# A graph network kernel on one core: register loads of window bases without their run-time bound check

## The chip, the cores and the metric

The kernel runs on one core of one Trainium2 chip. The metric is the time of one execution on the device in microseconds (us). Three runs of the kernel before took 7002.58, 7008.87 and 7010.35 us; their median is 7008.87 us.

## The reference

The input is a node matrix x (6250 nodes, 128 features, float32) and 206250 edges (src, dst), sorted by dst. Cut to what matters:

```python
def _L0_gnn_ref(x, edge_index, ...):
    row, col = (edge_index[0], edge_index[1])
    e_in = concatenate([x[row], x[col]], axis=-1)
    ef = relu(e_in @ ei_w1 + ei_b1) @ ei_w2 + ei_b2
    ew = sigmoid(ef @ ew_w + ew_b)[:, 0]
    out1 = _layernorm(gelu(_gcn(x, W1, b1, row, col, ew)), ln1_g, ln1_b)
    cat = concatenate([out1[row], out1[col], ef], axis=-1)
    ef = _layernorm(ef + (relu(cat @ eu_w1 + eu_b1) @ eu_w2 + eu_b2), lne_g, lne_b)
    ew = sigmoid(ef @ ew_w + ew_b)[:, 0]
    return _layernorm(gelu(_gcn(out1, W2, b2, row, col, ew)), ln2_g, ln2_b)
h = maximum(_layernorm(x), 0.0)
x = x + _L0_gnn_ref(h, ...)          # edge weights, two weighted sums over edges
h = maximum(_layernorm(x), 0.0)
x = x + _L1_gnn_ref(h, ...)          # an unweighted mean over edges, then a linear layer
```

`_gcn` takes for every destination node the sum over its edges of norm times the source node's row, where norm is the edge's weight times the inverse square roots of the weighted degrees of both ends.

## The kernel before, in words

The edges are cut into 404 groups of 512, and four groups make a step, so a pass over all edges has 101 steps. As the edges are sorted by destination, a group touches a short run of neighbouring destination nodes: a window of 32 nodes that begins at the group's base. The 404 bases lie as integers in one row, `base_sb`. Whoever reads a window from a table in HBM, or adds to a window of the accumulator `acc`, needs the base in a register of its own engine. `bases_of(eng, it)` (L830) loads the four bases of step `it` into registers of the engine `eng`; the library call behind it takes `min_val` and `max_val`.

The stages, in the order of the program, each ended by a barrier over all engines (`end_stage`, L326):

- setup: tables of node rows and the relative indices;
- **first edge round** (`edge_round(False)`, L835): for each group POOL issues four indirect DMAs (`gather_rows`, L791, L812) that gather the source rows of 128 edges each; ACT loads the group's destination window by DMA (`windows_of`, L1107), makes a one-hot matrix and TensorE (PE) multiplies it with the window (`q_of`, L1069); DVE adds, weighs and reduces to edge weights; SP writes the gathered rows to `kept_d`. ACT calls `bases_of` twice in a step, DVE once (L958), and DVE adds degrees into `acc` at the bases (`add`, L946);
- **first sum round** (`sum_kept_round`, L1212): the kept rows are read back, PE sums them by window, ACT copies the sums out of PSUM (`stage_folded`, L1287, L1290) and POOL calls `bases_of` once a step (L1408) and adds four windows into `acc` (L1413);
- the node update between the rounds;
- **second edge round** (`edge_round(True)`): the same gathers with wider rows; PE does `t_of`, `z_of` and `u_of` (L1003 to L1045) in turn, ACT does two relus for a group (`relus`, L1151: L1155 releases the matmul of `u_of` at L1029, L1158 releases `z_of`) and loads windows two steps ahead; ACT calls `bases_of` once a step, at the step's start (L1167), DVE once (L958);
- **second sum round**, and a node update;
- **count round** (`count_round`, L1424): 31 batches of 26 groups of 256 edges. DVE makes one-hots, PE counts and multiplies, ACT copies the 26 groups' sums to `staged_sums` (`stage_sums`, L1502, L1505), POOL loads the bases in fours (a load of its own, L1529, seven for a batch, the last of two) and adds 26 narrow windows one after the other (L1534), each waiting for the one before;
- the last linear layer.

POOL may issue gathers for a group once the group two steps earlier is used (`used`: L1029's semaphore in the second edge round, L892's in the first) and kept. The last step of a stage has no other work beside it: ACT stages the last sums, then POOL adds them, then the barrier comes.

Of the kernel before, what the change touches and what calls it, by code (L numbers as in the profile page):

```python
# [11 lines left out]
ds = bass.ds  # L12
SP = mybir.EngineType.SP
DVE = mybir.EngineType.DVE
POOL = mybir.EngineType.Pool
ACTE = mybir.EngineType.Activation

def build(nc, x, src, dst, W1, b1, W2, b2, ln1_g, ln1_b, ln2_g, ln2_b, ei_w1, ei_b1, ei_w2, ei_b2,
# [6 lines left out]
    NPAD = NT * P  # L25
# [4 lines left out]
    U = 4  # L30
# [4 lines left out]
    WIN = 32  # L35
    MAXR = N // WIN + 1
    NALL = NPAD + WIN
# [6 lines left out]
    CG = 26  # L44
# [16 lines left out]
    def done(i):  # L61

        return i + 1 + CREDIT

    ctx = ExitStack()
    with ctx:
# [113 lines left out]
        base_sb = sb("base_sb", [1, QG], I32)  # L180
# [649 lines left out]
        def bases_of(eng, it):  # L830

            return nc.values_load_multi_w_load_instructions(
                base_sb[0:1, ds(it * U, U)], engines=(eng,), min_val=0, max_val=NALL - WIN)[1]

        def edge_round(update):  # L835
            width = PR if update else ED
# [6 lines left out]
            with nc.Block() as block:  # L843
# [23 lines left out]
                def _(dve):  # L867
# [86 lines left out]
                    def step(it, par, k, behind, last):  # L954

                        if behind > 1:
                            keep_weights(it - 2)
                            firsts = bases_of(DVE, it - 2)  # L958
                        for u in range(U):
                            if update and not (last and u >= U - 2):  # L960
                                if u + 2 < U:
                                    hotT_of(it, par, k, u + 2)
                                else:
                                    hotT_of(it + 1, 1 - par, k + par, u + 2 - U)
                            if behind > 0 and u == U - 1:
                                weigh_hot(it - 1)
                            take_z(it, par, u)
                            if behind > 1 and u < 2:
                                add(it - 2, 2 * u, firsts[2 * u])
                                add(it - 2, 2 * u + 1, firsts[2 * u + 1])  # L970
                            if behind > 0 and u == 0:
                                hot_of(it - 1)
                            if behind > 0 and update and u == 1:
                                scale(it - 1)
                        if update:
                            variance(it)
# [17 lines left out]
                    for it in (STEPS - 2, STEPS - 1):  # L994
                        keep_weights(it)
                        firsts = bases_of(DVE, it)
                        for u in range(U):
                            add(it, u, firsts[u])
                            if it < STEPS - 1 and u == 0:
                                hot_of(it + 1)  # L1000
                                weigh_hot(it + 1)
# [101 lines left out]
                def _(act):  # L1103
# [13 lines left out]
                    def first_windows(it, par):  # L1117
                        firsts = bases_of(ACTE, it)
                        for u in range(U):
                            windows_of(it, par, u, firsts)  # L1120
# [303 lines left out]
        def count_round():  # L1424
# [3 lines left out]
            with nc.Block() as block:  # L1428
                @block.vector
                def _(dve):  # L1430
                    link = chain(dve, s_dve)
                    dve.sem_inc(s_hit, CREDIT)
                    link(nc.vector.tensor_scalar(rawz[:, :], rel[:, :], 0.0, None, ALU.is_ge))
                    link(nc.vector.scalar_tensor_tensor(rawz[:, :], rel[:, :], float(CW - 1), rawz[:, :],
                                                        ALU.is_le, ALU.mult))
                    link(nc.vector.tensor_tensor(code[:, :], srct[:, :], rel[:, :], ALU.add))
                    link(nc.vector.tensor_tensor(code[:, :], code[:, :], rawz[:, :], ALU.mult))
                    with dve.Fori(0, CB) as b:
                        for g in range(CG):
                            i = b * CG + g  # L1440
                            dve.wait_ge(s_built, done(i - 2))
                            for j in range(2):
                                nc.vector.tensor_scalar(hit_p[:, g % 2, j, :], part_ids[:, :],  # L1443
                                                        ew[:, ds(i * 2 + j, 1)], None, ALU.is_equal)
                                last = nc.vector.tensor_scalar(hit_c[:, g % 2, j, :], cell_ids[:, :],  # L1445
                                                               code[:, ds(i * 2 + j, 1)], None, ALU.is_equal)
                            last.then_inc(s_hit, 1)
# [73 lines left out]
                @block.gpsimd  # L1521
                def _(pool):
                    pool.sem_inc(s_acc, CREDIT + CG)

                    def batch(b, par):
                        pool.wait_ge(s_staged, done(b))
                        for g0 in range(0, CG, U):
                            n = min(U, CG - g0)
                            firsts = nc.values_load_multi_w_load_instructions(  # L1529
                                base_sb[0:1, ds(b * CG + g0, n)], engines=(POOL,), min_val=0, max_val=NPAD)[1]  # L1530
                            for g in range(g0, g0 + n):
                                a = acc[:, ds(firsts[g - g0], CW)]
                                pool.wait_ge(s_acc, done(b * CG + g - 1 + CG))
                                nc.gpsimd.tensor_tensor(a, a, staged_sums[:, par, g * CW:(g + 1) * CW],  # L1534
                                                        ALU.add).then_inc(s_acc, 1)
                    with pool.Fori(0, CB // 2) as q:
                        batch(2 * q, 0)
                        batch(2 * q + 1, 1)
                    batch(CB - 1, 0)
# [705 lines left out]
```

## Time and profile before

| | us |
|---|---|
| median of three runs | 7008.87 |
| lowest, highest | 7002.58, 7010.35 |
| span of the profiled execution | 8159.6 |
| first edge round in it (window 149 to 2665) | 2516 |
| first sum round (2714 to 3331) | 617 |
| second edge round (3437 to 6332) | 2895 |
| second sum round (6379 to 7018) | 639 |
| count round (7141 to 8114) | 973 |

The span is the only time the profiled execution gives; it is 1150.7 us above the median of the timed runs. Busy shares over the span are PE 59%, DVE 47%, POOL 45%, ACT 35%; no engine is busy throughout. Register instructions, waits and DMA issues don't count as busy; where they are shown, the engine's name has a q behind it (POOLq). The ends of matmuls are modelled.

### The profile page before, as it was taken

Reading aid. Unit: us, or ns where it says so; the run is one execution under the profiler, and the core shown is the slowest. Engines: PE = TensorE matmul, PEld = TensorE weight load, DVE = VectorE, ACT = ScalarE, POOL = GpSimd, SP = SyncE. Lnnn points to the kernel's source line nnn. Section 1 sums busy time; section 2 is a strip of 40 time slices with the busy share of each in tenths; the row PEclk is TensorE's granted clock in tenths of the full one; section 3 lists DMA queues with packets and bytes.
Section 4 is the critical chain, followed back from the end, with each engine's and each line's share of the span. In section 5 each row is a group of like instructions: output and inputs, shape, how many; then the busy total and the mean of one; then the engine's idle time right before and its main releaser. Section 6 shows DMA issues by size and latency. Waiting matters only on the chain. (4 is left out here: it accounts for less than half of the span.)

```text
span 8159.6 us, 171241 instructions
## 1 busy us (share of the span) xinstructions
PE 4819.1 (59%) x41016; PEld 3544.0 (43%) x41016; DVE 3862.8 (47%) x17284; ACT 2873.1 (35%) x5415; POOL 3652.2 (45%) x5091
## 2 busy tenths in 40 slices
PE   2111111111111588588888888888888588599997
PEld 1000000000000476455555555555555476478886
DVE  3222222222223788533333333333333688788886
ACT  2222222222222455322322222222223455566664
POOL 3566666666666011255555555555554011411222
PEclk6555555555555667777777777777778666699998
DMA  4455555555555477455555555555555577200000
GB/s 124 133 142 138 139 139 140 141 139 142 141 140 138 150 222 220 139 160 161 166 161 165 159 161 162 162 160 161 161 159 136 149 221 219 96 1 0 0 0 32
DMA packets 1010949, 1117.36 MB, mean 137 GB/s; under 512 B 216892, under 2 KB 749475, under 8 KB 1010440
## 3 DMA queue, kind: packets, MB, share of 16 engines
q1 hardware_dynamic: 652056, 516.07, 21.3%
q0 software_dynamic: 155136, 423.83, 19.7%
q10 hardware_dynamic: 203680, 176.57, 7.7%
q8 instruction: 31, 0.51, 0.0%
q14 instruction: 46, 0.38, 0.0%
HBM read 877.11 MB, written 238.87 MB: 137 GB/s over the span
## 5 line engine op out<-in xcount | busy, mean ns | idle before, releaser
L812 POOL DMA_INDIRECT counts<-tab_pr,idx x1616 | 1552.4, 961 | 1285.2 <-PE pu L1029 709.9
L812 POOL DMA_INDIRECT counts<-tab_p,idx x1616 | 1553.2, 961 | 926.5 <-issue 565.1
L1069 PE MATMUL pz<-tmpb,pieces 96*128 96x64 bf16 x1616 | 139.4, 236 | 2005.7 <-issue 1009.9
L1069 PEld LDWEIGHTS pz<-tmpb,pieces 96*128 96x128 bf16 x1616 | 94.7, 121 | 2077.9 <-issue 2077.9
L886 DVE BATCH_NORM_STATS2 st<-pz 128x6 f32<-128x64 f32 x1616 | 252.7, 219 | 1532.0 <-remote 850.2
L1029 PE MATMUL pu<-pieces,tmpb 96*128 96x512 f32 x808 | 628.9, 871 | 392.4 <-ACT pieces L1155 271.1
L892 DVE TENSOR_TENSOR pieces<-counts,pz 128x256 f32<-128x256 f32 x404 | 168.9, 418 | 1373.1 <-remote 1242.8
L1127 ACT ACTIVATE pieces<-pieces,iota_third 96x512 f32<-96x512 f32 x404 | 290.1, 718 | 1457.4 <-issue 1323.4
L1039 PE MATMUL pz<-wz,pieces 96*128 96x65 f32 x3232 | 732.9, 313 | 91.9 <-ACT pieces L1158 90.7
L1040 PE MATMUL pz<-wv,pieces 128*128 128x65 f32 x3232 | 713.8, 307 | 0.0
L1413 POOL TENSOR_TENSOR acc<-acc,pieces 128x32 f32 x808 | 199.7, 247 | 1124.9 <-issue 1018.8
L1470 PE MATMUL pz<-counts,pieces 128*128 128x286 bf16 x4557 | 682.5, 284 | 0.1
L1039 PEld LDWEIGHTS pz<-wz,pieces 96*128 96x128 f32 x3232 | 570.9, 221 | 214.3 <-ACT pieces L1158 114.4
L1158 ACT ACTIVATE pieces<-pu,eub 128x512 f32<-128x512 f32 x404 | 277.7, 687 | 1085.9 <-PE pu L1029 702.2
L1040 PEld LDWEIGHTS pz<-wv,pieces 128*128 128x128 f32 x3232 | 577.8, 223 | 0.0
L1445 DVE TENSOR_SCALAR pieces<-cell_ids,tmpb 128x540 bf16<-128x540 f16 x1612 | 572.1, 355 | 0.2 <-issue 0.2
L1534 POOL TENSOR_TENSOR acc<-acc,staged_sums 128x11 f32 x806 | 190.6, 236 | 785.6 <-issue 669.3
L1155 ACT ACTIVATE pieces<-pt 64x512 f32<-64x512 f32 x404 | 237.6, 588 | 775.4 <-remote 356.3
L1470 PEld LDWEIGHTS pz<-counts,pieces 128*128 128x128 bf16 x4557 | 442.0, 97 | 101.4 <-ACT counts L1497 0.4
L1443 DVE TENSOR_SCALAR pieces<-part_ids,ew 128x128 bf16<-128x128 bf16 x1612 | 407.4, 253 | 158.1 <-PE pt L1459 87.1
L1275 ACT ACTIVATE pieces<-counts,neg_p 128x512 f32<-128x512 bf16 x404 | 291.7, 722 | 491.0 <-DMA counts<-srcp_d 472.8
L1374 DVE SCALAR_TENSOR_TENSOR pieces<-iota_t,srct,pt 128x98 f32<-128x98 f32 x1616 | 399.6, 314 | 94.5 <-PE pt L1320 93.7
(318 smaller groups left out, 9906.9 us busy)
## 6 DMA issues: line engine op xcount, KB each, us to landing
kept_d<-counts SPq DMA_DIRECT2D x808, 256.0 KB
counts<-kept_d SPq DMA_DIRECT2D x808, 256.0 KB
pieces<-rel_d ACTq DMA_DIRECT2D x808, 192.0 KB
counts<-srcp_d SPq DMA_DIRECT2D x808, 64.0 KB
counts<-tab_p,idx POOLq DMA_INDIRECT x1616
counts<-tab_pr,idx POOLq DMA_INDIRECT x1616
tmpb<-tab_q ACTq DMA_DIRECT2D x808, 12.0 KB
tmpb<-tab_s ACTq DMA_DIRECT2D x404, 16.0 KB
```

The lines of the kernel that those rows point to most:

```text
L812: pool.indirect_dma_start(out=rows[:, par, u, j, 0:width], out_offset=None, in_=table, in_offset=bass.IndirectOffsetOnAxis(ap=idx[:, 2 * h ...
L886: nc.vector.bn_stats(st16[:, u * SUB + j, :], z[:, j, 0:ED])
L1029: nc.tensor.matmul(pu[u % 2][:, :], win[0:WE, par, u, :], tT[0:WE, u, :], start=False, stop=True, skip_group_check=True).then_inc(s_u, 1)
L1039: nc.tensor.matmul(o, tT[0:WE, u, j * P:(j + 1) * P], wz[0:WE, :], start=True, stop=False)
L1040: last = nc.tensor.matmul(o, uT[:, u % 2, j * P:(j + 1) * P], wv[:, :], start=False, stop=True)
L1127: nc.scalar.activation(apart, rel_row[:, par, u, :], ACT.Square, bias=iota_third[0:TRI, 0:1], scale=-1.0).then_inc(s_sq, 1)
L1158: nc.scalar.activation(uT[:, u % 2, :], pu[u % 2][:, :], ACT.Relu, bias=eub1[:, 0:1]).then_inc(s_urelu, 1)
L1275: nc.scalar.activation(dist, srcp_row[:, slot, :], ACT.Square, bias=neg_p[:, 0:1]).then_inc(s_sq, 1)
L1374: last = nc.vector.scalar_tensor_tensor(junk[:, u * SUB + j, :], iota_t[:, :], srct[:, ds(i * SUB + j, 1)], looked[u][:, j * HT:(j + 1) * ...
L1443: nc.vector.tensor_scalar(hit_p[:, g % 2, j, :], part_ids[:, :], ew[:, ds(i * 2 + j, 1)], None, ALU.is_equal)
L1445: last = nc.vector.tensor_scalar(hit_c[:, g % 2, j, :], cell_ids[:, :], code[:, ds(i * 2 + j, 1)], None, ALU.is_equal)
L1470: last = nc.tensor.matmul(pz[par][:, 0:CN], h3[:, k, t, :], counts[:, par, t, :], start=(t == 0 and k == 0), stop=(t == NT - 1 and k == 2))
```

## The change

Both calls that load bases into registers, `bases_of` (first and second edge round, sum rounds) and the load in `count_round`, get the argument that leaves out the check of each loaded value against `min_val` and `max_val` at run time. The loads stay, and so do all other instructions and their order.

```diff
         def bases_of(eng, it):
 
             return nc.values_load_multi_w_load_instructions(
-                base_sb[0:1, ds(it * U, U)], engines=(eng,), min_val=0, max_val=NALL - WIN)[1]
+                base_sb[0:1, ds(it * U, U)], engines=(eng,), min_val=0, max_val=NALL - WIN,
+                skip_runtime_bounds_check_because="next_windows and the end of a sum round clamp every base to NPAD")[1]
...
                             firsts = nc.values_load_multi_w_load_instructions(
-                                base_sb[0:1, ds(b * CG + g0, n)], engines=(POOL,), min_val=0, max_val=NPAD)[1]
+                                base_sb[0:1, ds(b * CG + g0, n)], engines=(POOL,), min_val=0, max_val=NPAD,
+                                skip_runtime_bounds_check_because="the end of a count round clamps every base to NPAD")[1]
```

In the program, a load of four bases is one TENSOR_LOAD, and eight sequencer instructions stand behind it (rows "ISA x8"): for each base one that compares (FUSED_REGOPS in the trace) and one that asserts (SEQ_ASSERT). The top of ACT's loop in the second edge round, before:

```order
L1190 UNCONDITIONAL_BRANCH
L1190 ISA
L832 TENSOR_LOAD base_sb
L832 ISA x8
L1153 ISA
L1154 REGISTER_ALU
L1155 ACTIVATE pieces<-pt 64x512
```

and with the change (its lines stand one or two further down):

```order
L1191 UNCONDITIONAL_BRANCH
L1191 ISA
L832 TENSOR_LOAD base_sb
L1154 ISA
L1155 REGISTER_ALU
L1156 ACTIVATE pieces<-pt 64x512
```

The eight instructions between the load and the first relu of the step are gone. POOL's loop in the count round, before:

```order
L1529 ISA
L1529 TENSOR_LOAD base_sb
L1529 ISA x8
L1533 REGISTER_ALU
L1534 ISA
L1534 TENSOR_TENSOR acc<-acc,staged_sums 128x11
```

and with the change:

```order
L1530 ISA
L1530 TENSOR_LOAD base_sb
L1535 REGISTER_ALU
L1536 ISA
L1536 TENSOR_TENSOR acc<-acc,staged_sums 128x11
```

Here the eight stood between the load and the first add of each four. On no engine does any other instruction appear, vanish or change its place.

## Rows read from the trace of the kernel before

**Rows 1.** Head of the profile page.

```profile
span 8159.6 us, 171241 instructions
```

**Rows 2.** By stretch: length, PE, PEld, DVE, ACT, POOL busy; PEclk, DMA share, GB/s.

```profile
149.00:2665.00 2516.00, 326.83 (x2828) 168.50 (x2828) 692.45 (x1919) 568.02 (x910) 1564.52 (x1667) 0.50 0.53 140
...
3437.00:6332.00 2895.00, 2388.84 (x11716) 1638.54 (x11716) 1049.74 (x4351) 830.73 (x1213) 1563.56 (x1667) 0.75 0.57 160
7141.00:8114.00 973.00, 936.24 (x7781) 752.80 (x7781) 772.18 (x3228) 586.26 (x1644) 190.61 (x806) 0.98 0.00 0
```

**Rows 3.** Instructions of L832: count, min/median/max ns, first and last start.

```profile
L832 ACTq SEQ_ASSERT  x1208: 1/18/1400, 150.5 to 6257.7; - x173
...
L832 DVEq FUSED_REGOPS  x808: 7/190/1392, 237.8 to 6329.3; - x162
```

**Rows 4.** Instructions of L1529, same columns.

```profile
L1529 POOLq FUSED_REGOPS  x1016: 51/147/162, 7205.3 to 8112.1; - x170
L1529 POOLq SEQ_ASSERT  x806: 18/18/24, 7206.0 to 8112.3; - x162
```

**Rows 5.** POOL's adds at the end of the count round, timeline (start, us).

```profile
8095.69 0.21 POOL L1534 TENSOR_TENSOR acc<-acc,staged_sums 128x11 f32 x1 [0.17 <-POOL acc L1534]
...
8110.23 0.21 POOL L1534 TENSOR_TENSOR acc<-acc,staged_sums 128x11 f32 x1 [1.19 <-issue]
...
8112.89 0.21 POOL L1534 TENSOR_TENSOR acc<-acc,staged_sums 128x11 f32 x1 [0.17 <-POOL acc L1534]
```

**Rows 6.** ACT's last staging copy of the count round, timeline.

```profile
8091.82 0.41 ACT L1505 ACTIVATE staged_sums<-pz 128x286 f32<-128x286 f32 x1 [17.79 <-PE pz L1470]
```

**Rows 7.** End of the first sum round, ACT and POOL, timeline.

```profile
3325.93 0.28 ACT L1290 ACTIVATE pieces<-pd 128x128 f32<-128x128 f32 x1 [1.17 <-PE pd L1342]
...
3327.78 0.24 POOL L1413 TENSOR_TENSOR acc<-acc,pieces 128x32 f32 x1 [0.17 <-POOL acc L1413]
3329.20 0.25 POOL L1413 TENSOR_TENSOR acc<-acc,pieces 128x32 f32 x1 [1.17 <-issue]
```

**Rows 8.** DVE at the ends of the two edge rounds, timeline.

```profile
2658.77 0.18 DVE L952 TENSOR_TENSOR acc<-acc,pd 33x32 f32 x1 [1.19 <-PE pd L1057]
...
6326.66 0.69 DVE L938 TENSOR_TENSOR pieces<-pieces,wts 128x512 f32<-128x512 bf16 x1
```

**Rows 9.** ACT's last sigmoid of the second edge round, timeline.

```profile
6325.62 0.31 ACT L1148 ACTIVATE wts<-zl,zb 128x16 f32<-128x16 f32 x1
```

**Rows 10.** Instructions of L812, count, min/median/max ns, first and last start.

```profile
L812 POOL DMA_INDIRECT counts<-tab_p,idx x1616: 943/949/1455, 150.8 to 2639.9; - x180
L812 POOL DMA_INDIRECT counts<-tab_pr,idx x1616: 943/949/1467, 3438.7 to 6285.7; - x180
```

**Rows 11.** One gather of POOL in the first edge round, timeline.

```profile
1500.81 0.95 POOL L812 DMA_INDIRECT counts<-tab_p,idx  x1 [0.30 <-issue]
```

**Rows 12.** Who waited for whom: us in total, times, longest us.

```profile
POOL counts L812 <- PE pu L1029: 709.9, 221, 6.5
...
PEld pu L1029 <- ACT pieces L1155: 285.2, 92, 6.5
```

**Rows 13.** A step's boundary in the second edge round, ACT, timeline.

```profile
5004.15 0.69 ACT L1158 ACTIVATE pieces<-pu,eub 128x512 f32<-128x512 f32 x1 [2.60 <-PE pu L1029]
5004.30 0.32 ACTq L1109 DMA_DIRECT2D pieces<-rel_d  x1
...
5007.17 0.59 ACT L1155 ACTIVATE pieces<-pt 64x512 f32<-64x512 f32 x1 [2.33 <-issue]
```

**Rows 14.** PE at the same boundary, timeline.

```profile
5001.71 1.08 PE L1029 MATMUL pu<-pieces,tmpb 96*128 96x512 f32 x2
...
5007.81 2.08 PE L1029 MATMUL pu<-pieces,tmpb 96*128 96x512 f32 x2 [0.92 <-ACT pieces L1155]
```

**Rows 15.** Two stretches of the second edge round, columns as rows 2.

```profile
5160.00:5440.00 280.00, 237.81 (x1128) 163.61 (x1128) 100.02 (x419) 79.93 (x117) 151.11 (x161) 0.73 0.57 159
5440.00:5720.00 280.00, 229.41 (x1167) 156.24 (x1166) 103.63 (x431) 82.49 (x121) 155.31 (x165) 0.79 0.58 163
```

## The prediction

> **What bounds the kernel now.** First the times: the profiled execution spans 8159.6 us [rows 1], the runs take 7008.9, so 1150.7 us of the span are not in the runs, and I must say where they lie before I price anything. The sum below is made as differences, which I subtract from the median. The views by stretch [rows 2] show two edge rounds of 2516 and 2895 us; all the rest is 8159.6 - 5411 = 2748.6 us. If the rest is as long in the runs, both edge rounds together take 7008.9 - 2748.6 = 4260 us there.
>
> Next, the floor of an edge round. POOL issues 1616 gathers in each [rows 10], each 0.95 us long with 0.30 us before the next [rows 11]: 1616 x 1.25 = 2020 us. The first starts 1.8 us into each window of rows 2, and the last starts 25 us (2665 - 2639.9) and 46 us (6332 - 6285.7) before the end, so the two rounds can't be shorter than 4040 + 4 + 71 = 4115 us. The runs have 4260: they go nearly at POOL's pace, and at most about 145 us are waits of POOL. In the profile it waits much more, in the second round 709.9 us for the matmul of L1029 alone [rows 12]. I read this as: the edge rounds are POOL's in the runs, with a remainder in the second round, where PE and ACT are coupled. The count round is PE's (936 of 973 us busy, [rows 2]), with POOL behind it; at the end of each stage the last engine works alone.
>
> **The price of a check.** Each loaded base costs one comparison and one assertion on its engine's instruction stream: 147 + 18 ns on POOL [rows 4]; on DVE the comparison is 190 ns, and ACT's assertion is 18 ns too [rows 3]. Four bases are thus at least 4 x 0.165 = 0.66 us. From above: an add of POOL behind a load waits 1.19 us against 0.17 without one [rows 5], so load and checks together add 1.02 us. I take 0.9 us for four, since the load runs largely beside the add before it, and 1.0 on DVE. The change removes 1208 checked values on ACT [rows 3], 808 on DVE, 808 on POOL in the sum rounds and 806 on POOL in the count round [rows 4]: by 0.225 us each over 800 us of instruction stream. Hardly any of it sets an end, as follows. It removes nothing else, adds nothing, and moves no DMA past a queue.
>
> These instructions don't occupy the compute part: while ACT's relu runs from 5004.15 for 0.69 us, its stream already issues a DMA at 5004.30 [rows 13]. The Trainium skill, "Perfetto Trace Analysis", section "Per-instruction lifecycle", says the same of DVE and ACT: the stream hands an instruction to a wait queue and goes on to the next one. By that rule alone, a check behind a running instruction would be free wherever the engine has a queue of work; the sum would then be the ends of the stages only, which is my second rival.
>
> **Count round.** The checks are 5.9 us for a batch (26 values). In the steady state POOL waits for the next batch, and they cost nothing: PE covers them, and would if they were twice as long. At the end they don't hide. ACT has staged the last sums at 8091.82 + 0.41 = 8092.2 [rows 6], POOL finishes the batch before at 8095.69 + 0.21 = 8095.9, then does the last one until 8113.1 [rows 5]. Without checks the earlier batch is 5.9 us shorter, so the last starts at 8092.2 (3.7 us earlier) and is itself 5.9 shorter: -9.6 us. Late next is ACT's copy.
>
> **Sum rounds.** POOL has one load in a step of 6.1 us (617 / 101) and waits in the steady state; DVE, PE and the row reads cover it, so 0. At the end the last sums are staged at 3325.93 + 0.28 = 3326.2, POOL ends the step before at 3327.78 + 0.24 = 3328.0, and its next add is held 1.17 us [rows 7]. Two earlier steps without checks remove the 1.8 us of backlog, the last saves 0.9; since the load already runs beside the add before it, I take 2.5 us. Two rounds: -5.0 us.
>
> **Ends of the edge rounds.** DVE loads bases for the last two steps, and for one more while it still has groups to do. In the first round two such loads lie in DVE's chain (1.19 us before the add at 2658.77 [rows 8] is one): -2.0 us. The third is followed by a wait for PE's last sums and gives nothing. In the second round the weighing at 6326.66 [rows 8] follows the sigmoid that ends at 6325.93 [rows 9], so only 0.7 can come off. Together -2.7 us. At the start ACT's loads have two steps of POOL's work (40 us) before anyone misses them: 0.
>
> The ends sum to 9.6 + 5.0 + 2.7 = **-17.3 us**, to 6991.6.
>
> **Edge rounds, steady.** First round: in a step ACT drops the checks of eight values (1.8 us), DVE of four (1.0 us), of the 20 us that POOL takes. PE is busy for 13% of it. Taken at 0. Second round: ACT's load stands between the window DMAs and the first relu of a step (L1155), which L1029 needs. At 5007.17 this relu starts after 2.33 us idle, and PE waits 0.92 us for it [rows 13, 14]: about what the checks take. If that held for all 101 steps it would be 91 us. PE's weight load at L1029 waits for L1155 in 92 of 404 groups [rows 12], 23%. I take 0.23 x 101 x 0.9 = -21 us; the bounds are 0 and -91. The release of POOL by L1029 then comes earlier, and late next are POOL's own gathers. DVE's checks I cost at nothing: PE doesn't wait for DVE in these rows.
>
> Forecast: 7008.9 - 17.3 - 21 = 6970.6, **6971 us** (-0.54%). About 0.2% (14 us) is what a measurement of this kernel can tell from no change.
>
> **The rivals.**
> 1. *The relief is whole.* The check on ACT costs every step of the second round its 0.9 us, because the granted clock rises with it. For it: the same matmul is recorded with 1.08 us and, around the wait of 0.92, with 2.08 [rows 14], and the mean granted clock is only 0.75 of the 2.4 GHz, a mixture of the two levels [rows 2]. Against it: at most 145 us of POOL's waits are there to win. The time is 6991.6 - 91 = 6901 us, with the whole remainder of both rounds 6991.6 - 110 = 6882. The Trainium skill, "TensorE: Matmul & The Clock Gate", Part 1, has the clock depend on how busy the engine recently was; by that rule a gap that closes pays twice, which the two durations at rows 14 agree with, and the time would be this one. Chance 0.14.
> 2. *Only the ends.* POOL's pace hides the second round too: 6992 us. For it: the runs are near the floor. Chance 0.22; the boundary of 0.2% is 6994.9, so a small error in my ends makes it "same".
> 3. *Nothing that shows.* The ends are half as long without the recording, -8 us: 7001 us. Against it: adds, loads and checks at the ends have regular, short records. Chance 0.08.
> 4. *Slower.* PE and POOL in the second round get out of a rhythm: ACT asks for windows earlier, PE is done sooner within a step, waits in one longer piece for gathers, and the granted clock falls. The price: at clock 0.79 PE starts 1167 matmuls in 280 us, at 0.73 it is 1128 [rows 15], 3.5% for 0.06. A fall by 0.03 costs 1.7% of a round of some 2130 us, 36 us: 6991.6 + 36 = 7028 us. It decides from a fall of 0.015 on, where it eats the ends. Against it: in the runs POOL's pace, not PE's, sets most steps. Chance 0.06.
>
> That the change doesn't do what it says is excluded: the assertions are gone from the built program.
>
> **How the numbers follow.** The forecast has 0.50. Faster by over 0.2% come the forecast, rival 1 and 0.12 of rival 2: 0.76. Same: 0.10 of rival 2 and rival 3: 0.18. Slower: 0.06. The range is 6885 to 7006: it takes in rivals 2 and 3, rival 1 to nearly its end, and leaves out the slower one.
>
> **What would show it.** No SEQ_ASSERT in any stage; the adds behind a load in the count round about 0.3 us after the one before instead of 1.19; from the end of ACT's last L1505 to the end of POOL's last L1534 11.3 us, now 20.9; from the end of the last L1290 to the end of the last L1413 about 2.0 us, now 4.5. In the second edge round fewer waits of L1029 for L1155. The span may fall more than the runs, since in it ACT's stream was late in the first round and POOL waited. Wrong would be: a median above 6995 with both ends shortened (the steady part gives nothing), or a second edge round with a lower granted clock and longer steps (rival 4); a gain above 110 us would mean that the edge rounds are not at POOL's pace in the runs.

## The result and the profile after

| | us |
|---|---|
| changed kernel, median of nine runs | 6988.72 (6976.05 to 6993.65) |
| kernel before, median of nine runs beside them | 7007.86 (7000.76 to 7020.7) |
| ratio, 95% interval | 0.9967 (0.9959 to 0.9975) |
| span of the changed kernel's profiled execution | 6985.6 |
| span of the kernel before, profiled again in the experiments | 7007.8 |

The kernel is 0.33% faster: 19 us between the medians, 23 by the ratio. The profiled execution with the 8159.6 us [rows 1] was disturbed, by what no run shows; the kernel before, profiled once more, spans 7007.8 us like its runs. So the comparisons below are with that second profile, and what of [rows 2 to 15] it doesn't repeat is named.

First the register side. Instructions of the load's line in the three helpers, changed kernel (count, min/median/max ns, first and last start):

```profile
L832 ACTq TENSOR_LOAD <-base_sb x302: 303/311/1157, 151.5 to 5099.3; - x151
L832 DVEq TENSOR_LOAD <-base_sb x202: 340/346/1145, 197.7 to 5170.7; - x101
L832 POOLq TENSOR_LOAD <-base_sb x202: 315/319/348, 2355.0 to 5853.4; - x101
```

The 1208 assertions of ACT and the 808 comparisons of DVE [rows 3] have no row any more; the loads themselves have stayed. The same for the count round's load:

```profile
L1530 POOLq TENSOR_LOAD <-base_sb x217: 315/510/957, 6041.6 to 6938.1; - x109
L1530 POOLq FUSED_REGOPS  x210: 51/51/65, 6041.5 to 6924.5; - x105
```

Of 1016 FUSED_REGOPS [rows 4] 210 are left, the short ones of 51 ns, so 806 comparisons and 806 assertions are gone. The load takes 510 ns in the median and up to 957, against 315 at best.

By stretch, changed kernel (columns as rows 2; the edge rounds, and the count round last):

```profile
150.00:2278.00 2128.00, 337.46 (x2828) 170.72 (x2828) 712.32 (x1919) 567.25 (x910) 1579.07 (x1667) 0.50 0.59 165
...
3051.00:5175.00 2124.00, 1975.32 (x11716) 1372.92 (x11716) 1069.34 (x4351) 827.67 (x1213) 1561.82 (x1667) 0.94 0.77 218
5977.00:6940.00 963.00, 934.87 (x7781) 752.27 (x7781) 768.69 (x3228) 585.83 (x1644) 181.48 (x806) 0.99 0.00 0
```

And the kernel before, profiled again:

```profile
149.00:2280.00 2131.00, 337.25 (x2828) 170.97 (x2828) 711.17 (x1919) 567.17 (x910) 1581.91 (x1667) 0.50 0.59 165
3051.00:5182.00 2131.00, 1968.11 (x11716) 1365.60 (x11716) 1062.62 (x4351) 827.85 (x1213) 1567.75 (x1667) 0.93 0.77 217
5989.00:6962.00 973.00, 935.23 (x7781) 752.41 (x7781) 771.89 (x3228) 586.24 (x1644) 190.31 (x806) 0.98 0.00 0
```

The second edge round of the kernel before takes 2131 us, not 2895 [rows 2], and its granted clock is 0.93 of 2.4 GHz, not 0.75. The two edge rounds sum to 4262 us, where the prediction had worked out 4260. The count round is 10 us shorter now, the second edge round 7, the first 3. Of these only the 10 us can be read from one pair of profiles: an edge round of unchanged code differs by up to 10 us from one profile to the next (see "Why the prediction was right or wrong", 7 and the account).

The end of the count round, changed kernel, timeline of ACT's last staging copy:

```profile
6928.00 0.41 ACT L1506 ACTIVATE staged_sums<-pz 128x286 f32<-128x286 f32 x1 [17.80 <-PE pz L1471]
```

and POOL behind it:

```profile
6925.69 0.20 POOL L1536 TENSOR_TENSOR acc<-acc,staged_sums 128x11 f32 x1 [0.17 <-POOL acc L1536]
6928.95 0.21 POOL L1536 TENSOR_TENSOR acc<-acc,staged_sums 128x11 f32 x1 [3.06 <-ACT staged_sums L1506]
...
6935.37 0.21 POOL L1536 TENSOR_TENSOR acc<-acc,staged_sums 128x11 f32 x1 [0.27 <-POOL acc L1536]
...
6939.15 0.21 POOL L1536 TENSOR_TENSOR acc<-acc,staged_sums 128x11 f32 x1 [0.17 <-POOL acc L1536]
```

POOL has ended the batch before and waits 3.06 us for the copy: its backlog is gone. An add behind a load follows 0.27 us after the one before, where it was 1.19 [rows 5]. From the end of the copy (6928.41) to the end of the last add (6939.36) it is 10.95 us. The kernel before, second profile, copy and last add:

```profile
6940.26 0.41 ACT L1505 ACTIVATE staged_sums<-pz 128x286 f32<-128x286 f32 x1 [17.79 <-PE pz L1470]
...
6961.29 0.21 POOL L1534 TENSOR_TENSOR acc<-acc,staged_sums 128x11 f32 x1 [0.17 <-POOL acc L1534]
```

There the copy ends at 6940.67 and the last add at 6961.50, which is 20.83 us.

The end of the first sum round, changed kernel, ACT and POOL:

```profile
2941.05 0.28 ACT L1291 ACTIVATE pieces<-pd 128x128 f32<-128x128 f32 x1 [2.01 <-PE pd L1343]
...
2941.88 0.25 POOL L1414 TENSOR_TENSOR acc<-acc,pieces 128x32 f32 x1 [1.31 <-ACT pieces L1291]
...
2943.13 0.24 POOL L1414 TENSOR_TENSOR acc<-acc,pieces 128x32 f32 x1 [0.17 <-POOL acc L1414]
```

Kernel before, second profile, the same place:

```profile
2938.92 0.28 ACT L1290 ACTIVATE pieces<-pd 128x128 f32<-128x128 f32 x1 [2.00 <-PE pd L1342]
2940.66 0.25 POOL L1413 TENSOR_TENSOR acc<-acc,pieces 128x32 f32 x1 [1.28 <-issue]
...
2941.92 0.24 POOL L1413 TENSOR_TENSOR acc<-acc,pieces 128x32 f32 x1 [0.17 <-POOL acc L1413]
```

Copy end to last add is 2.04 us now and 2.96 before, 0.92 less: the four checks of one load. In [rows 7] it had been 4.5, because POOL was a step behind in that execution.

The end of the second edge round: ACT's last sigmoid, DVE's weighing behind it, and DVE's last add. Changed kernel:

```profile
5168.93 0.31 ACT L1149 ACTIVATE wts<-zl,zb 128x16 f32<-128x16 f32 x1
5169.27 0.69 DVE L939 TENSOR_TENSOR pieces<-pieces,wts 128x512 f32<-128x512 bf16 x1 [0.52 <-ACT wts L1149]
...
5174.10 0.18 DVE L953 TENSOR_TENSOR acc<-acc,pd 1x32 f32 x1 [0.20 <-DVE acc L953]
```

Kernel before, second profile:

```profile
5175.37 0.31 ACT L1148 ACTIVATE wts<-zl,zb 128x16 f32<-128x16 f32 x1
5176.41 0.69 DVE L938 TENSOR_TENSOR pieces<-pieces,wts 128x512 f32<-128x512 bf16 x1
...
5181.25 0.18 DVE L952 TENSOR_TENSOR acc<-acc,pd 1x32 f32 x1 [0.20 <-DVE acc L952]
```

Before, the last sigmoid ended at 5175.68 and the weighing began 0.73 us later; now it ends at 5169.24 and the weighing begins 0.03 us later, released by ACT. That is the 0.7 us of the prediction.

The waits in the second edge round (total us, times, longest us), changed kernel:

```profile
PEld pu L1030 <- ACT pieces L1156: 54.1, 70, 2.5
...
POOL counts L812 <- PE pu L1030: 16.8, 37, 1.0
```

Kernel before, second profile:

```profile
PEld pu L1029 <- ACT pieces L1155: 156.5, 180, 5.4
...
POOL counts L812 <- PE pu L1029: 15.3, 29, 1.1
```

These four lines hold the lesson of the case. PE waits 102 us less for ACT's relu, about one microsecond for each of the 101 steps, near the 91 us of the upper bound. And POOL, which sets the time, waited 15 us for PE before and waits 17 now: the 102 us were slack, nearly all of them. The other profiles below say the same. PE's wait for the relu is 156 to 173 us in the six undisturbed ones with ACT's checks as in the kernel before and 54 to 62 in the four without; POOL's wait for PE is 15 to 27 us in the six (mean 22.8) and 16 to 23 in the four (mean 18.5). In the disturbed execution that last wait was 709.9 us [rows 12].

### The profile page after: what moved, and what is told of

Read it like the earlier page. It is cut to its first block and busy times, and to the rows that moved or that the text cites. A ratio compares the mean times of both kernels' runs of the same rounds, so it can differ in the third digit from the quotient of the medians.

```text
span 6985.6 us, 163981 instructions
## 1 busy us (share of the span) xinstructions
PE 4437.6 (64%) x41016; PEld 3300.6 (47%) x41016; DVE 3899.3 (56%) x17284; ACT 2869.6 (41%) x5415; POOL 3655.2 (52%) x5091
## 5 line engine op out<-in xcount | busy, mean ns | idle before, releaser
L812 POOL DMA_INDIRECT counts<-tab_p,idx x1616 | 1567.9, 970 | 534.2 <-issue 487.2
L812 POOL DMA_INDIRECT counts<-tab_pr,idx x1616 | 1548.4, 958 | 534.0 <-issue 483.9
L1132 ACT ACTIVATE pieces<-pieces 96x512 bf16<-96x512 f32 x404 | 254.6, 630 | 1176.1 <-PE pz L1070 1172.0
L1040 PE MATMUL pz<-wz,pieces 96*128 96x65 f32 x3232 | 664.2, 288 | 0.8 <-ACT pieces L1159 0.8
L1041 PE MATMUL pz<-wv,pieces 128*128 128x65 f32 x3232 | 643.4, 282 | 0.0
L1040 PEld LDWEIGHTS pz<-wz,pieces 96*128 96x128 f32 x3232 | 506.3, 197 | 100.6 <-issue 98.3
L1041 PEld LDWEIGHTS pz<-wv,pieces 128*128 128x128 f32 x3232 | 508.7, 198 | 0.0
L1030 PE MATMUL pu<-pieces,tmpb 96*128 96x512 f32 x808 | 469.7, 665 | 44.1 <-ACT pieces L1156 43.7
L1128 ACT ACTIVATE pieces<-pieces,iota_third 96x512 f32<-96x512 f32 x404 | 289.9, 718 | 300.6 <-issue 214.8
```

The lines of the kernel that those rows point to most:

```text
L812: pool.indirect_dma_start(out=rows[:, par, u, j, 0:width], out_offset=None, in_=table, in_offset=bass.IndirectOffsetOnAxis(ap=idx[:, 2 * h ...
L1030: nc.tensor.matmul(pu[u % 2][:, :], win[0:WE, par, u, :], tT[0:WE, u, :], start=False, stop=True, skip_group_check=True).then_inc(s_u, 1)
L1040: nc.tensor.matmul(o, tT[0:WE, u, j * P:(j + 1) * P], wz[0:WE, :], start=True, stop=False)
L1041: last = nc.tensor.matmul(o, uT[:, u % 2, j * P:(j + 1) * P], wv[:, :], start=False, stop=True)
L1128: nc.scalar.activation(apart, rel_row[:, par, u, :], ACT.Square, bias=iota_third[0:TRI, 0:1], scale=-1.0).then_inc(s_sq, 1)
L1132: nc.scalar.activation(hotT3[:, u, :], apart, ACT.Relu, bias=1.0, scale=-1.0).then_inc(s_hotT, 1)
```

## The experiments

Two views stand against each other: that a check costs time only where its engine has the last work of a stage (it is a matter of place), and that ACT's checks in the second edge round cost time in every step as well. All ratios are to the kernel before in runs on the same chip. Where the file has an extra statement ahead of a line, that line's number in the profile is larger.

**The kernel before once more**, to learn what its profile shows when undisturbed.

> The kernel before once more, for a second profiled execution. The profile of before spans 8159.6 us against runs of 7009; the changed kernel's spans 6985.6 against 6989. Theory A (the long profile was one disturbed execution): span 6995 to 7020, first edge round about 2130 us and second about 2125, as in the changed kernel, POOL waiting for neither L892 nor L1029. Theory B (the checks cost much in the edge rounds when recorded): span about 8160 again, edge rounds 2516 and 2895. Ratio to before 1.000 in both.

Measured: 7003.83 us beside 7000.59, ratio 1.0002 (0.9993 to 1.0011); span 7007.8. Its rows stand above. The disturbed execution was an exception, and everything that the prediction read from its waits in the second edge round has to be read again.

**The change in the count round alone.**

```
@@ count_round, batch
-                                base_sb[0:1, ds(b * CG + g0, n)], engines=(POOL,), min_val=0, max_val=NPAD)[1]
+                                base_sb[0:1, ds(b * CG + g0, n)], engines=(POOL,), min_val=0, max_val=NPAD,
+                                skip_runtime_bounds_check_because="every base is clamped to NPAD")[1]
```

> Checks left out in the count round alone. Ends theory: -9.6 us, ratio 0.9986; the time from the end of ACT's last copy to POOL's last add falls from 21 to 11.3 us, the steady batches stay 30 us. Steady theory (all the gain is in the second edge round): 0.

Measured: 6992.43 us, 0.9986 (0.9977 to 0.9995). Copy end to last add 11.24 us, the stage 964.4 us against 973.5. This part is the one whose gain stands outside the noise by itself.

**In the sum rounds alone** (POOL's use of `bases_of`).

```
@@ bases_of
-                base_sb[0:1, ds(it * U, U)], engines=(eng,), min_val=0, max_val=NALL - WIN)[1]
+                base_sb[0:1, ds(it * U, U)], engines=(eng,), min_val=0, max_val=NALL - WIN,
+                skip_runtime_bounds_check_because="every base is clamped to NPAD" if eng == POOL else None)[1]
```

> Checks left out on POOL in the two sum rounds alone. Ends theory: -5.0 us, ratio 0.9993; from the end of the last staging copy to POOL's last add 2.0 us instead of 4.5 in each round. Rival (POOL's adds pace the sum rounds): each of 101 steps gives 0.9 us, -180 us.

Measured: 6997.66 us, 0.9995 (0.9986 to 1.0004). Copy end to last add is 2.04 and 2.03 us, against 2.96 twice. The backlog of [rows 7] does occur elsewhere, but not as a rule: with POOL's checks behind the wait, seven undisturbed profiles have fourteen such ends, of which eleven take 2.96 or 2.97 us and three, all of the second sum round, 3.68, 3.69 and 4.32.

**In the edge rounds alone** (ACT's and DVE's use).

```
-                skip_runtime_bounds_check_because="every base is clamped to NPAD" if eng == POOL else None)[1]
+                skip_runtime_bounds_check_because="every base is clamped to NPAD" if eng != POOL else None)[1]
```

(shown against the edit before)

> Checks left out on ACT and DVE in the two edge rounds alone. POOL's pace hides the steady state: -2.7 us from the ends, ratio 0.9996, steady steps at 20.1 us in both rounds. Forecast of the prediction: -24 us, ratio 0.9966. Whole relief: -94 us.

Measured: 6994.70 us, 0.9995 (0.9986 to 1.0004). PE's waits for ACT's relu fall as in the changed kernel, and POOL's don't follow:

```profile
PEld pu L1030 <- ACT pieces L1156: 61.8, 81, 1.9
...
POOL counts L812 <- PE pu L1030: 22.9, 49, 1.0
```

So the condition on which the predicted 21 us hung was met, and the 21 us didn't come. The three parts multiply to 0.9986 x 0.9995 x 0.9995 = 0.9976, against 0.9967 for all of them; each interval is 0.0009 wide to either side, so this neither shows nor excludes that the parts help one another.

**The changed kernel again**, and two kernels in which the load moves and the checks stay or go. In the first, every check of the kernel before is still executed, but POOL's are ahead of the wait for the staged sums:

```
@@ sum_round, step
-                        pool.wait_ge(s_staged, done(it))
                         firsts = bases_of(POOL, it)
+                        pool.wait_ge(s_staged, done(it))
@@ count_round, batch
+                        firsts = nc.values_load_multi_w_load_instructions(
+                            base_sb[0:1, ds(b * CG, CG)], engines=(POOL,), min_val=0, max_val=NPAD)[1]
                         pool.wait_ge(s_staged, done(b))
-                        for g0 in range(0, CG, U):
-                            n = min(U, CG - g0)
-                            firsts = nc.values_load_multi_w_load_instructions(
-                                base_sb[0:1, ds(b * CG + g0, n)], engines=(POOL,), min_val=0, max_val=NPAD)[1]
-                            for g in range(g0, g0 + n):
-                                a = acc[:, ds(firsts[g - g0], CW)]
+                        for g in range(CG):
+                            a = acc[:, ds(firsts[g], CW)]
...
```

The second has the same move in the changed kernel.

> The changed kernel again, beside the others of this call. The parts alone gave 0.9986, 0.9995 and 0.9995. If they add up: ratio 0.9976 (-17 us). If more is gained together than alone (the first timing, 0.9967): 0.9967. Edge rounds by stage within 10 us of the kernel before.

> All checks kept, but on POOL the bases are loaded and checked before the wait for the staged sums: in the sum rounds the load goes above the wait, in the count round one load of 26 bases with its 26 checks stands above it. Ends theory (a check costs only where it stands behind the last wait): the end of the count round 21 -> about 10.2 us, of the sum rounds 2.96 -> about 1.7 each, -13 us, ratio 0.998, although POOL executes every check. Work theory (what counts is how much POOL's stream executes): 0, ratio 1.000.

> The changed kernel with the same hoisting of POOL's loads. Ends theory: the loads alone were 0.32 us in each sum round's end and about 2 us at the count round's end, so 2 to 3 us below the changed kernel, ratio about 0.9973 to the kernel before, 0.9963 if the changed kernel is at 0.9967. Count end 10.2 us, sum ends 1.7 us.

Measured, beside 7017.97 us of the kernel before:

| | us | ratio | count end | sum ends |
|---|---|---|---|---|
| changed kernel again | 6994.28 | 0.9968 (0.9956 to 0.9981) | 10.95 | |
| checks kept, moved ahead of the wait | 6991.81 | 0.9962 (0.9949 to 0.9976) | 9.79 | 1.67, 3.01 |
| no checks, moved too | 6991.21 | 0.9962 (0.9949 to 0.9976) | 9.77 | 1.66, 1.66 |

(ends: from the last staging copy to POOL's last add, us). The end of the count round with all checks kept:

```profile
6921.02 0.20 POOL L1532 TENSOR_TENSOR acc<-acc,staged_sums 128x11 f32 x1 [0.17 <-POOL acc L1532]
6929.75 0.21 POOL L1532 TENSOR_TENSOR acc<-acc,staged_sums 128x11 f32 x1 [8.53 <-ACT staged_sums L1505]
...
6939.16 0.21 POOL L1532 TENSOR_TENSOR acc<-acc,staged_sums 128x11 f32 x1 [0.17 <-POOL acc L1532]
```

Between the last two batches POOL has 8.53 us until the copy comes, and the checks of 26 values fit into it. From the copy on, 26 adds follow in 9.6 us. For POOL in the count round this settles that the place decides: all 1614 checks of POOL (808 and 806) are executed, and the end is as short as in the kernel that has none (9.79 and 9.77 us). Being ahead of the wait doesn't make a check free in every case. The second sum round with the checks moved ends in 3.01 us, not 1.67: its last two copies end 1.94 us apart, POOL takes 2.70 us from the first add of one step to the first of the next there, and so the last step's first add starts 1.50 us after the copy. The kernel without checks and with the move has the lowest median of the three, but none of them can be told from the others.

One number of this table is more than the ends explain. With the checks moved, the ends are shorter by 11.0 us (count) and 1.3 us (first sum round), 12 us together, but the ratio says 27 us (17 to 36 by its interval), and ACT and DVE still do all their checks in it. So a gain beyond the ends, 15 us by these numbers, comes also without taking anything off the edge rounds. What it is stays open.

**Doubling**, to see how much slack each engine's load has in the edge rounds. The base is the kernel before; a second load of the same four values, with its checks, is put ahead of ACT's:

```
@@ bases_of
+            for _ in range(1 if eng == ACTE else 0):
+                nc.values_load_multi_w_load_instructions(
+                    base_sb[0:1, ds(it * U, U)], engines=(eng,), min_val=0, max_val=NALL - WIN)
             return nc.values_load_multi_w_load_instructions(
```

> The kernel before, but ACT loads and checks its bases twice in both edge rounds: 1.25 us more of ACT's stream for a load, 2.5 us in a step of the first round, 1.25 in the second. POOL's pace hides it: 0 to +3 us, ratio 1.000. Forecast's reading (23% of the steps' boundaries miss ACT's time): 0.23 x 101 x 1.25 = +29 us, 1.0041. Whole: +126 us, 1.018.

Measured: 7238.86 us beside 7017.97, 1.0311 (1.0297 to 1.0325), by far the largest effect in the case. The first edge round, where ACT does this twice in a step, took 2137 us (2131); the second took 2362.7 (2131.0), 2.3 us more for each of its 101 steps. Added were 1.4 us: from the start of the first load to the end of the last assertion ACT's stream takes 2.70 us in the mean of the steps of the second round, where it was 1.28. The second edge round of this kernel:

```profile
3053.00:5416.00 2363.00, 2051.98 (x11716) 1405.46 (x11716) 1054.05 (x4351) 828.25 (x1213) 1558.04 (x1667) 0.87 0.70 196
```

and its waits:

```profile
PEld pu L1032 <- ACT pieces L1158: 317.4, 193, 8.7
...
POOL counts L812 <- PE pu L1032: 289.9, 169, 2.6
```

PE's waits for the relu double (156.5 before), and now they go through: POOL waits 289.9 us for PE. The granted clock is 0.87 instead of 0.93, and PE is busy for 84 us more with the same 11716 matmuls, 0.8 us a step; with the 1.4 us added that comes to the 2.3. One boundary of a step in this kernel (PE):

```profile
4008.69 1.79 PE L1032 MATMUL pu<-pieces,tmpb 96*128 96x512 f32 x2 [1.75 <-ACT pieces L1158]
```

and two boundaries, one step apart, in the kernel before, second profile:

```profile
4003.04 1.93 PE L1029 MATMUL pu<-pieces,tmpb 96*128 96x512 f32 x2 [0.86 <-ACT pieces L1155]
...
4023.62 1.13 PE L1029 MATMUL pu<-pieces,tmpb 96*128 96x512 f32 x2 [0.52 <-ACT pieces L1155]
```

Over the 4 us from 4008.6 the granted clock is 0.57 of 2.4 GHz in this kernel, that is mostly at the lower of its two levels (1.2 GHz); in the kernel before it is 0.57 over the 4 us from 4003.0 and 1.00 from 4023.6. So the slow pair isn't new; it comes more often. Of the 404 pairs at this line 93 take over 1.6 us with ACT twice, 59 in the kernel before and 34 in the changed kernel; of these 89, 44 and 11 belong to the first group of a step. The Trainium skill, "TensorE: Matmul & The Clock Gate", Part 1, has the clock depend on how busy the engine was just before; by that rule a longer gap costs its own length and then slower matmuls, which agrees with 2.3 us lost for 1.4 added. That the clock carries the rest is read from these rows; it wasn't isolated.

Three kernels were then to ask whether it is the engine, the amount or the place. DVE twice with checks (the same edit with `eng == DVE`); ACT twice, the extra load without its checks; and the extra checked load at another point of ACT's step in the second edge round:

```
                             if update and left > 2:
                                 windows_of(it + 2, par, u, firsts)
+                                if u == 1:
+                                    bases_of(ACTE, it + 2)
```

> The kernel before, but DVE loads and checks its bases twice in both edge rounds, 1.4 us more of DVE's stream in a step. ACT twice cost 2.3 us in each step of the second round and nothing in the first. Theory PE-ACT loop (only the chain from relu to L1029 to relu is tight; DVE has slack): 0 in both rounds, ratio 1.000. Rival (in the second round any engine's stream is tight): +1.4 to +2.5 us a step, +140 to +250 us there.

> The kernel before, but ACT loads its bases once more without checks: 0.35 us more at the step's start. ACT's 1.25 more cost +232 us in the second round (2.3 us a step). Threshold theory (the loop of PE and ACT is just under POOL's step of 20.8 us and costs only what it is over): between 0 and +60 us. Proportional theory: 0.35/1.25 x 232 = +65 us, ratio 1.009.

> The kernel before, but in the second edge round ACT loads and checks its bases a second time after the windows of the step's second group, not at the step's start: the same 1.25 us more in a step as ACT twice, at a boundary of groups that has no load yet. Place theory (what counts is the gap between the relu that ends one group and the first relu of the next, and the gap at the step's start was the longest): under +30 us. Amount theory (ACT's whole stream in a step counts): about +230 us as before, ratio 1.032.

Measured, beside 7014.12 us of the kernel before:

| | us | ratio | second edge round | POOL waits for PE |
|---|---|---|---|---|
| DVE twice | 7019.03 | 1.0005 (0.9995 to 1.0015) | 2137.8 | 22.1 |
| ACT, load alone (not executed, see below) | 7016.82 | 1.0004 (0.9994 to 1.0013) | 2131.4 | 21.6 |
| ACT, other place | 7082.49 | 1.0101 (1.0080 to 1.0121) | 2206.9 | 102.5 |

The middle row says nothing about the amount. Instructions on ACT of the added call (L833) and of the call that was there (L835), and then ACT's added load in the kernel with ACT twice:

```profile
L833 ACTq FUSED_REGOPS  x147: 51/56/76, 175.5 to 5118.0; - x147
L835 ACTq TENSOR_LOAD <-base_sb x302: 304/312/1093, 150.9 to 5118.1; - x151
```

```profile
L833 ACTq TENSOR_LOAD <-base_sb x302: 304/507/1097, 150.1 to 5344.2; - x151
```

The added load without checks, whose value nobody uses, has no TENSOR_LOAD in the trace: ACT has the 302 of the kernel before and the same number of instructions. This row is the kernel before once more.

The waits of the last one:

```profile
PEld pu L1029 <- ACT pieces L1155: 203.3, 253, 4.6
...
POOL counts L812 <- PE pu L1029: 102.5, 113, 2.6
```

The slack is then known from two sides. On DVE a load with four checks can be added without effect. On ACT, ahead of the window transfers, another load with its checks (1.4 us) cost 232 us, and in the middle of the step (1.3 us) it cost 76 us, 0.75 us a step. Taking the checks away at the head of the step, 0.9 us, gave about 3 us (below). So what is taken off the head of ACT's step gives hardly anything, and somewhere between nothing and 1.4 us more the time begins to rise; where, no run shows.

## Why the prediction was right or wrong

The measured 6988.7 us is within the range, but the sum behind the forecast was not right: of its -38 us the largest term, -21, hardly came. The time is near that of rival 2, "only the ends" (6992), and the ends were smaller than in it too; that it lies 3 us below, by the ratio (-23 us) 6, is in part a gain that no one has placed. The range was wide enough for all of this.

1. **Reading past the disturbed profile: right.** That the missing 1150 us lay in the edge rounds, and that these take 4260 us at POOL's pace, is what the second profile shows (2131.6 + 2131.0 us from barrier to barrier). The "at most about 145 us" of waits of POOL were hardly waits, though: in the second round of that profile POOL's idle time ahead of its gathers is 508.2 us of its own issue, 15.3 us for PE and 9.1 us for DMA. POOL's gathers, kernel before, second profile:

```profile
L812 POOL DMA_INDIRECT counts<-tab_p,idx x1616: 942/946/1462, 150.9 to 2265.1; - x180
L812 POOL DMA_INDIRECT counts<-tab_pr,idx x1616: 942/946/1486, 3053.1 to 5153.3; - x180
```

2. **The price of a check: right.** Four cost 0.92 us at the end of a sum round (0.9 taken).

3. **The end of the count round, -9.6: right.** It measured 20.83 to 10.95, -9.9, and the stage as a whole fell from 973.5 to 962.6 us. Late next was ACT's copy, as said.

4. **The ends of the sum rounds, -5.0: mis-sized.** They gave 0.92 each, -1.8 together. The step that failed is "Two earlier steps without checks remove the 1.8 us of backlog": in eleven of fourteen undisturbed ends there was no backlog to remove.

5. **The ends of the edge rounds, -2.7: nearly right.** From the last gather's start to DVE's last add the first round went from 14.7 to 13.6 us, -1.1 (I had counted two loads in the chain; one lay in it). In the second round 0.7 came off at the weighing, as predicted.

6. **First edge round, steady, 0: right.** Over all undisturbed profiles it takes 2128 to 2138 us, with no order by whether ACT checks.

7. **Second edge round, steady, -21: this was the step that failed.** "I take 0.23 x 101 x 0.9" let every wait of PE for the relu count as time of the round. The share itself was even too low in an undisturbed execution (180 of 404 groups, not 92), and the wait did go, 102 us of it. But POOL sets the round, and it waits 15 us for PE in all. The number to price by was POOL's wait, which the disturbed execution had at 709.9 us. From first to last gather the round takes 2095.2 to 2103.0 us in the six profiles with ACT's and DVE's checks (mean 2099.2; one of them has DVE's twice) and 2094.0 to 2097.4 in the four without (mean 2095.9): about -3, with ranges that overlap. The Trainium skill, "Perfetto Trace Analysis", section "Per-instruction lifecycle", has the stream of DVE and ACT hand its instructions to a wait queue ahead of their execution, from which the prediction had rival 2. The time came near that of rival 2, but not in this way: the checks did hold ACT's relus back, as PE's wait for them fell by 102 us, and what hid them was POOL's pace. Rival 1's "whole remainder" of 110 us comes from no row, and no run shows it.

8. **Rival 4, slower by the granted clock: did not come.** With less work on ACT the clock is 0.94 (0.93 before); it was more work on ACT that went with a lower one, 0.87.

The account: -10 (count), -1.8 (sum rounds), -1.8 (ends of the edge rounds), -3 (second round) is -17; measured are -19 to -23. The rest could lie in the second edge round too: as a whole it takes 2123.5 to 2127.8 us in the four profiles without checks (mean 2126.0) and 2128.6 to 2138.5 in the six with them (mean 2134.3), 8 us apart. Five of the 8 lie behind the last gather, where the profiles with checks take anything from 26 to 41 us and those without 27.5 to 28.6. Whether the checks cause these longer ends, or few samples make it look so, stays open. The kernel with POOL's checks moved speaks for caution: it keeps ACT's and DVE's checks, its ends account for 12 us, and its ratio says 27.

## What to carry to other kernels

A profile whose span isn't that of the runs can still tell durations and orders, but not waits: profile again before a wait is priced. A wait that goes is worth what the engine that sets the stage waits less, not what the engine next in line does; here 102 us of PE's waits gave about 3. Work on an instruction stream is priced by where it stands against the last wait: moved ahead of it the checks of the count round cost nothing that shows, while behind it those of the last two batches cost 10 us. If a check is wanted for safety, moving it was as good as dropping it here, as long as the engine has time before the wait. And an experiment that adds work is read only after the trace has shown that the work was executed.

## What the runs showed that I had not expected

- The second edge round is lopsided: taking 0.9 us off ACT's step gives about nothing, adding 1.4 costs 2.3 us a step, more than was added, while PE's granted clock goes from 0.93 to 0.87.
- One more load with its checks cost 232 us ahead of the window transfers and 76 us between them; on DVE nothing.
- A second load without checks, whose values were not used, left no TENSOR_LOAD in the trace.
- POOL's register load of four values takes 510 ns in the median and up to 957 ns in the count round, with or without checks, while in the sum rounds it stays within 315 to 348.
